# Projection in split halves from the sixth tile on, one row buffer for attention and norms, and three steps of each tile moved

## What is computed

```python
def attention(q, k, v, W_proj, b_proj):            # 16 heads of 32
    scores = einsum('bhqd,bhkd->bhqk', qh, kh) / sqrt(32)
    scores = where(abs(i - j) > 64, -inf, scores)  # window of 64 to each side
    y = einsum('bhqk,bhkd->bhqd', softmax(scores), vh)
    return y @ W_proj.T + b_proj

def ffn(x):                                        # scan over the 8 batches, c is 512 x 512
    f = sigmoid(x_t @ wf.T + c @ uf.T + bf)
    i = sigmoid(x_t @ wi.T + c @ ui.T + bi)
    g = tanh(x_t @ wc.T + c @ uc.T + bc)
    c = f * c + i * g                              # for each batch t
    return tanh(x @ wo.T + c_final @ uo.T + bo)

x = x + attention(layernorm(x), ctx, ctx, W_proj, b_proj)
x = x + ffn(layernorm(x))
```

## Time and profile before

| | |
|---|---|
| median of 3 runs | 1033.33 us |
| profiled execution, its own time | 1036.05 us |
| its span | 1034.3 us |
| PE, DVE, ACT, POOL busy | 97%, 59%, 47%, 18% |
| granted TensorE clock, mean | 0.991 of full |
| DMA | 99.36 MB, 96 GB/s over the span |

### The profile page before, as it was taken

One profiled execution on the slowest core, in us unless ns is written; L12 is line 12 of the kernel. 1 busy time (PEld: TensorE's weight loads), 2 busy tenths in 40 slices (PEclk: granted clock), 3 DMA queues, 4 the chain that ended last, 5 costly groups with the idle time before them and its releaser, 6 DMA issues.

```text
span 1034.3 us, 20027 instructions
## 1 busy us (share of the span) xinstructions
PE 1005.1 (97%) x6992; PEld 728.0 (70%) x6992; DVE 610.2 (59%) x2194; ACT 485.0 (47%) x1441; POOL 188.4 (18%) x289
## 2 busy tenths in 40 slices
PE   6998989999999999999999999999999999999997
PEld 4665656667776777767777777767777778888885
DVE  5757878776567755766676655765577632133222
ACT  6757656555454454554455445454454432131221
POOL 4535111101111111111111111111111000002354
PEclk9988999999999999999999999999999999999999
DMA  8346223222222122212222222211112003029666
GB/s 265 119 134 189 84 76 98 83 77 73 77 83 58 61 77 83 60 49 72 78 83 77 72 77 70 70 52 47 41 33 72 1 23 131 0 84 364 245 214 193
DMA packets 76244, 99.36 MB, mean 96 GB/s; under 512 B 5232, under 2 KB 46192, under 8 KB 74608
## 3 DMA queue, kind: packets, MB, share of 16 engines
q1 hardware_dynamic: 75424, 97.80, 29.7%
q10 hardware_dynamic: 720, 0.27, 0.1%
HBM read 68.69 MB, written 29.36 MB: 95 GB/s over the span
## 4 chain that ended last, share of the span: by engine, by line
PE 89%; DVE 4%; issue 2%; DMA 2%; ACT 1%; POOL 1%; SPq 0%; DVEq 0%; POOLq 0%; ACTq 0%
PE ps_g L474 16%; PE ps_g L472 16%; PE ps_g L473 16%; PE ps_m L569 12%; PE ps_a L508 6%; PE ps_a L527 4%; PE ps_v L548 3%; PE ps_m L575 2%; PE ps_v L553 2%; PE ps_g L520 2%; PE ps_m L562 2%; PE ps_a L472 1%; PE ps_a L473 1%; PE ps_a L474 1%; PE ps_m L483 1%
## 5 line engine op out<-in xcount | busy, mean ns | idle before, releaser
L727 DVE CUSTOM_DVE_ANT_0 probs<-ps_a,mask 128x192 f32<-128x192 f32 (+1 forms) x512 | 169.4, 387 | 193.1 <-PE ps_a L508 146.3
L641 ACT ACTIVATE probs<-probs,rowmin 128x192 f32<-128x192 f32 (+1 forms) x512 | 239.0, 471 | 1.8 <-DVE rowmin L727 1.8
L676 ACT ACTIVATE gate<-ps_g,bias 128x512 f32<-128x512 f32 x84 | 57.9, 689 | 216.7 <-PE ps_g L474 216.7
L750 DVE STREAM_TRANSPOSE probs_t<-probs 32x128 f32<-32x128 f32 x492 | 146.6, 298 | 6.0
L472 PE MATMUL ps_g<-state_hi,gate_w 128*128 128x512 f32 x336 | 145.5, 433 | 0.0
L646 ACT ACTIVATE probs_t<-ps_a 128x512 f32<-128x512 f32 x108 | 64.5, 597 | 153.6 <-PE ps_a L527 152.9
L474 PE MATMUL ps_g<-state_hi,gate_w 128*128 128x512 f32 x336 | 132.3, 394 | 0.0
L473 PE MATMUL ps_g<-state_lo,gate_w 128*128 128x512 f32 x336 | 131.2, 391 | 0.0
L456 POOL COPY recip<-invsum 128x128 f32<-128x128 f32 x128 | 38.5, 301 | 503.0 <-DVE invsum L734 503.0
L569 PE MATMUL ps_m<-wp,attn 128*128 128x512 f32 x256 | 121.6, 619 | 0.0
L641 ACT ACTIVATION_READ_ACCUMULATOR probs<-probs,rowmin 128x1 f32 x512 | 97.6, 191 | 0.0
(11 more groups left out here) (167 smaller groups left out, 1599.5 us busy)
## 6 DMA issues: line engine op xcount, KB each, us to landing
values<-ctx_rows SPq DMA_DIRECT2D x34, 256.0 KB, 4.3
xr<-x SPq DMA_DIRECT2D x32, 256.0 KB, 4.0
keys<-ctx_t SPq DMA_DIRECT2D x16, 512.0 KB, 4.0
x_dram<-xr SPq DMA_DIRECT2D x32, 256.0 KB, 4.2
gate_w<-x2t_dram SPq DMA_DIRECT2D x8, 1024.0 KB, 11.2
keys<-ctx_t SPq DMA_DIRECT2D x16, 384.0 KB, 3.4
x2t_dram<-x2t_even SPq DMA_DIRECT2D x12, 512.0 KB, 3.8
x2t_dram<-x2t_odd SPq DMA_DIRECT2D x12, 512.0 KB, 3.8
```

Of the source, the lines that this page charges most:

```text
L641: act.activation(row, row, ACT.Exp, bias=rowmin[:, i % 2, h:h + 1], scale=-1.0, accum_out=rowsum[:, i // G % 2, i % G, h:h + 1]).then_inc( ...
L676: act.activation(gate[:, min(gt, 1), :], ps_g[i % 2][:, :], ACT.Tanh, bias=(first_bias if b == 0 else bias)[:, gt, m:m + 1], scale=1.0 if ...
L727: dve.tensor_tensor_reduce(probs[:, i % 2, h, 0:SEEN[t]], ps_a[h][:, 0:SEEN[t]], mask[:, MASK0[t]:MASK0[t] + SEEN[t]], -SCALE, -NEG, ALU.a ...
L750: turn = dve.transpose(probs_t[BLK * keys_of:BLK * (keys_of + 1), HPG:2 * HPG, q], probs[q, i % 2, :, col:col + BLK])
```

## The change

Of the projections, those of tiles 5 to 31 (`WHOLE` is 5) are made in split halves. For that the projection's weights are split once, in slots 19 and 20 (`split_proj`: four ACT copies, four POOL subtractions), and each tile's attention is split behind `mult` (a new step `halves`: ACT rounds it into `attn_hi`, POOL subtracts into `attn_lo`). The raw projection weights lie where the recurrent state is kept later, so the first state waits for both. `xn`, `x2` and `attn` become one buffer, `tile_row`, and `queries` has one half only; the waits follow. In the later slots (n > 19) `query`, `turn2` and `spread` move from the end of slots 1, 2 and 3 to right behind `turn`, ACT's copy of the query stands behind `exp` as a step of its own (`query_out`), and `mult` goes from the start of the next tile to slot 3, in front of `exp` and `value`. `stat2` stands right behind `resid` in all slots (so in front of the maskings), and `ln2b` behind the `score` of slot 1.

```diff
@@ -56,6 +56,8 @@
 
     FIRST_CELL = G * TT + 3
     OWN_BANKS = FIRST_CELL + 1
+
+    WHOLE = OWN_BANKS // G
     XR = 4
     PAIR = 2
     chunks = [(gt, u, k) for u in (1, 0) for gt in range(NG) for k in range(0, G, PAIR)]
@@ -119,7 +121,7 @@
 
     steps += [("load_x", 0), ("load_k", 0), ("load_x", 1), ("load_v", 0), ("load_x", 2)]
     steps += [("load_k", 1), ("load_v", 1)]
-    steps += [("ln1", 0), ("ln1b", 0), ("bias", 0), ("query", 0), ("ln1", 1)]
+    steps += [("ln1", 0), ("ln1b", 0), ("bias", 0), ("query", 0), ("query_out", 0), ("ln1", 1)]
     steps += [("score", 0), ("score", 1), ("exp", 0), ("recip", 0)]
     split_slots = [1 + 3 * c // 2 for c in range(NCH)]
 
@@ -135,22 +137,29 @@
         if n + 1 in split_slots:
             steps.append(("load_w", split_slots.index(n + 1)))
         early = n <= FIRST_CELL
-        if s == 0 and n > FIRST_CELL + 1:
-            tile_steps("mult", i - 1)
         if s == 1 and early:
             tile_steps("resid", i - 1)
+            tile_steps("stat2", i - 1)
         if n < SLOTS:
             steps.append(("turn", n))
         if early:
             steps.append(("exp", n + 1))
         else:
+            if s > 0:
+                tile_steps((None, "query", "turn2", "spread")[s], (None, i + 1, i - 1, i)[s])
             cells(2)
         if n + 2 < SLOTS:
             steps.append(("score", n + 2))
+        if s == 1:
+            tile_steps("ln2b", i - 1)
+        if s == 3 and not early:
+            tile_steps("mult", i)
         if early:
             tile_steps(("proj", "query", "turn2", "spread")[s], (i - 1, i + 1, i - 1, i)[s])
         elif n + 1 < SLOTS:
             steps.append(("exp", n + 1))
+        if s == 1:
+            tile_steps("query_out", i + 1)
         if n < SLOTS:
             steps.append(("value", n))
         gates()
@@ -164,23 +173,18 @@
             if not early:
                 tile_steps("proj", i - 1)
                 tile_steps("resid", i - 1)
+                tile_steps("stat2", i - 1)
             tile_steps("load_k", i + 2)
             tile_steps("load_v", i + 1) if i > 0 else None
-        if s == 1:
-            tile_steps("stat2", i - 1)
-            if not early:
-                tile_steps("query", i + 1)
-            tile_steps("ln2b", i - 1)
         if s == 2:
-            if not early:
-                tile_steps("turn2", i - 1)
             tile_steps("load_x", i + 3)
             tile_steps("ln1", i + 2)
-        if s == 3:
-            if early:
-                tile_steps("mult", i)
-            else:
-                tile_steps("spread", i)
+        if s == 3 and early:
+            tile_steps("mult", i)
+        if s == 3 and i >= WHOLE:
+            tile_steps("halves", i)
+        if FIRST_CELL <= n < FIRST_CELL + 2:
+            steps.append(("split_proj", PAIR * (n - FIRST_CELL)))
         if n in split_slots:
             steps.append(("split", split_slots.index(n)))
         if n == 0:
@@ -227,18 +231,24 @@
         x2t = [x2t_even, x2t_odd]
         state_hi = sb("state_hi", [P, G, T], F32R)
         state_lo = sb("state_lo", [P, G, T], F32R)
-        wp = sb("wp", [P, G, D], F32)
+        proj_w = sb("proj_w", [P, 2, G, D], F32R)
+
+        wp = state
         xr = sb("xr", [P, XR, D], F32)
-        xn = sb("xn", [P, D], F32)
-        x2 = sb("x2", [P, D], F32)
-        queries = sb("queries", [P, 2, G, P], F32)
+
+
+        tile_row = sb("tile_row", [P, D], F32)
+        xn = x2 = tile_row
+        attn = tile_row[:, :].rearrange("p (g q) -> p g q", g=G)
+        queries = sb("queries", [P, G, P], F32)
         keys = sb("keys", [P, 2, G, KEYS], F32)
         values = sb("values", [P, 2, 2, D], F32)
         probs = sb("probs", [P, 2, HPG, KEYS], F32)
 
         probs_t = sb("probs_t", [P, 2 * HPG, P], F32)
         recip = sb("recip", [P, G, P], F32)
-        attn = sb("attn", [P, G, P], F32)
+        attn_hi = sb("attn_hi", [P, G, P], F32R)
+        attn_lo = sb("attn_lo", [P, G, P], F32R)
         gate = sb("gate", [P, 2, T], F32)
         mask = sb("mask", [P, MASKW], F32)
         ident = sb("ident", [P, P], F32)
@@ -450,6 +462,16 @@
                         pool.wait_ge(w_hi, PAIR * i + k - k0 + 1)
                         pool.tensor_tensor(gate_w[:, gt, u, 1, k, :], raw_w[i % RAW][:, k - k0, :],
                                            gate_w[:, gt, u, 0, k, :].bitcast(F32), ALU.subtract).then_inc(w_lo, 1)
+                if kind == "split_proj":
+                    for k in range(i, i + PAIR):
+                        pool.wait_ge(wp_hi, k + 1)
+                        pool.tensor_tensor(proj_w[:, 1, k, :], wp[:, k, :], proj_w[:, 0, k, :].bitcast(F32),
+                                           ALU.subtract).then_inc(wp_lo, 1)
+                if kind == "halves":
+                    pool.wait_ge(attn_round, i - WHOLE + 1)
+                    need(pool, projected, i)
+                    pool.tensor_tensor(attn_lo[:, :, :], attn, attn_hi[:, :, :].bitcast(F32), ALU.subtract)\
+                        .then_inc(attn_split, 1)
                 if kind == "recip":
                     pool.wait_ge(inverted, i + 1)
                     need(pool, spread, i // G)
@@ -505,7 +527,7 @@
                         mm.then_inc(column, 1)
                     for h in range(HPG):
                         rows = slice(HEAD * h, HEAD * (h + 1))
-                        mm = pe.matmul(ps_a[h][:, 0:seen], queries[rows, tile % 2, g, :], keys[rows, tile % 2, g, 0:seen],
+                        mm = pe.matmul(ps_a[h][:, 0:seen], queries[rows, g, :], keys[rows, tile % 2, g, 0:seen],
                                        start=True, stop=True)
                     mm.then_inc(scored, 1)
                 if kind == "turn":
@@ -564,9 +586,16 @@
                 if kind == "proj":
                     if i == 0:
                         pe.wait_ge(wp_in, DMA)
-                    pe.wait_ge(attn_t, i + 1)
-                    for k in range(G):
-                        mm = pe.matmul(ps_m[:, :], attn[:, k, :], wp[:, k, :], start=(k == 0), stop=(k == G - 1))
+                    if i < WHOLE:
+                        pe.wait_ge(attn_t, i + 1)
+                        for k in range(G):
+                            mm = pe.matmul(ps_m[:, :], attn[:, k, :], wp[:, k, :], start=(k == 0), stop=(k == G - 1))
+                    else:
+                        pe.wait_ge(wp_lo, G)
+                        pe.wait_ge(attn_split, i - WHOLE + 1)
+                        for k in range(G):
+                            mm = product(ps_m[:, :], (attn_hi[:, k, :], attn_lo[:, k, :]),
+                                         (proj_w[:, 0, k, :], proj_w[:, 1, k, :]), k == 0, k == G - 1)
                     mm.then_inc(projected, 1)
                 if kind == "turn2":
                     pe.wait_ge(x2_done, i + 1)
@@ -628,10 +657,10 @@
             for gt in range(NG):
                 act.dma_start(bias[:, gt, :], biases[gt]).then_inc(const_in, DMA)
             for kind, i in steps:
-                if kind == "query":
+                if kind == "query_out":
                     act.wait_ge(q_turned, i + 1)
-                    need(act, scored, G * (i - 1))
-                    act.activation(queries[:, i % 2], ps_m[:, :].rearrange("p (g q) -> p g q", g=G), ACT.Copy)\
+                    need(act, scored, G * i)
+                    act.activation(queries[:, :, :], ps_m[:, :].rearrange("p (g q) -> p g q", g=G), ACT.Copy)\
                        .then_inc(q_ready, 1)
                 if kind == "exp":
                     need(act, inverted, i - 2 * G + 1)
@@ -647,9 +676,16 @@
                        .then_inc(turned_a, 1)
                 if kind == "spread":
                     act.wait_ge(spread, i + 1)
+                    act.activation(attn, ps_m[:, :].rearrange("p (g q) -> p g q", g=G), ACT.Copy).then_inc(recip_out, 1)
+                if kind == "halves":
+                    act.wait_ge(attn_t, i + 1)
                     need(act, projected, i)
-                    act.activation(attn[:, :, :], ps_m[:, :].rearrange("p (g q) -> p g q", g=G), ACT.Copy)\
-                       .then_inc(recip_out, 1)
+                    act.activation(attn_hi[:, :, :], attn, ACT.Copy).then_inc(attn_round, 1)
+                if kind == "split_proj":
+                    if i == 0:
+                        act.wait_ge(wp_in, DMA)
+                    for k in range(i, i + PAIR):
+                        act.activation(proj_w[:, 0, k, :], wp[:, k, :], ACT.Copy).then_inc(wp_hi, 1)
                 if kind == "turn2":
                     b, t = i // TT, i % TT
                     act.wait_ge(x2_turned, i + 1)
@@ -708,6 +744,10 @@
                     r = i % 2
                     dve.wait_ge(rstd1, i + 1)
                     need(dve, q_turned, i)
+                    if i - 2 < WHOLE:
+                        need(dve, projected, i - 1)
+                    else:
+                        dve.wait_ge(attn_split, i - 1 - WHOLE)
```

(8 more changed lines are left out.)

2 lines of the change are left out of this document (added).

## The result

The changed kernel took 1020.35 us (median of 4 runs, 1014.17 to 1022.76), against 1034.05 us before: ratio 0.985 [0.982, 0.988], a gain of 13.7 us and not of 28.7. The time lies 3 us above the range. The four executions differ in the first 110 us above all: the profiled one is the fastest (1014.17 us, span 1012.4, mean clock 0.995), and the slowest (1022.76 us) has a clock of 0.990.

The account below looks back on a forecast made before the run. TensorE bounds the kernel, wholly so from 179 us; gains of 21.8 (third regime), 2.7 (second) and 4.2 us (first) make 28.7, taken from the profiled 1036.05 and lowered to the runs' median: 1005 us, range 995 to 1017.

Parts of the forecast that it names:

- Rival A: Third regime: new chain partly late, 0.3 to 0.8 us of each tile's 0.87 lost to waits; 1017 us, chance 0.15.
- rival C: Slower: mult too late, so mult, ACT and POOL come bare, 2.9 us per tile; 1076 us, chance 0.03.
- Rival D: Split products don't run in 0.23 us; from 0.30 us a step nothing is saved there; 1026 us, chance 0.03.
- 3.63 - 2.76 = 0.87 us per tile: Third regime (from 179 us): saving of the split projection, twelve rounded products at 2.76 us for the old 3.63.
- 20.9 us: Forecast gain from projection 8 to the end: projections 8 to 31, 24 x 0.87 us.
- 1.3 us for the third tile: First regime: weights land at 84.16, so the value product comes at 85.8 and not 87.13, gaining 1.3 us.
- 2.5 for the fourth: First regime: no transfer in the way, so the 1.84 us wait and 0.7 of low clock are gained.
- the second tile, where I set the gain to none: First regime: no gain, since ACT then stands 2.81 us for the weights' transfer.
- Rival B: Low clock of the first two regimes goes altogether and DVE's gaps close: 36 us gained, 998 us, chance 0.17.
- 3.6 forecast: Gain from projection 4 to 8: 2.7 us for the second regime and 0.87 of projection 7.
- about 1 us: Second regime: the early spread waits about 1 us for the maskings, blends and reciprocal of the slot before.
- 0.3 to 0.5 us to spare: Query's transposes behind the turn of slot 1: residual and norm of slot 0 ready 0.3 to 0.5 us ahead.

Follow-up runs that it names:

- `mult` late: Changed kernel with the spread back at the end of slot 3 and mult, then halves, at the start of the next tile: 1036.18 us, ratio 1.001.
- the cell that took them over: Changed kernel with one cell of slot 0 put between the value product and the split projection: 1020.76 us, ratio 0.987.
- the columns: Changed kernel with weights' transfers a slot earlier, and one first-bias column per score instead of two, started a slot earlier: 1007.00 us, ratio 0.972.
- the whole projection: Changed kernel with all projections in full precision, no weights or attention split, moved steps and shared row buffer kept: 1038.16 us, ratio 1.003.

## Why the prediction was wrong

**Right: where the gain lies, and that nothing of it is lost to waits in the third regime.** PE bounds the kernel, the split projection is nearly all of the gain (816 for 832 to 833 us; without it nothing), the halves hide behind the maskings and the value product, and the subtraction took 1.29 us for the estimated 1.27. Rival A, chain partly late, did not come: PE has no gap from 196 to 850 us. That the measured 1020.35 lies in rival A's range (1012 to 1025) is chance, since its mechanism is not there. Of rival C a late chain is real with `mult` late, at 0.5 us per tile and not 2.9, and the change avoids that place. Rival D is excluded by the steps of 0.23.

**Wrong by size: "3.63 - 2.76 = 0.87 us per tile".** The 2.76 was read off twelve products that begin behind the query's transposes, which had already paid for the passage from the narrow products. The projection stands right behind the narrow products, and what stood there in the profile before was the projection itself, so that the 3.63 held the passage and the 2.76 did not. The chain gives 2.95 us, a saving of 0.68; the way from projection 8 to the end gives 0.67 to 0.71 per tile, the length of a batch 0.66. Of 20.9 us that leaves 16.1 to 16.9. That the 0.20 belong to the place is shown by the cell that took them over; that they are the load of a 128-wide stationary operand which can't begin beside the 32-column products is what the load rows suggest, and no run shows it by itself. The Trainium skill (TensorE: Matmul & The Clock Gate, The mechanism) has a load run ahead beside a matmul when it goes to other rows of the array or to a background buffer; the loads beside the products of 0.23 us, each 0.39 us ahead, agree.

**Wrong in the first regime: 1.3 us for the third tile, 2.5 for the fourth.** This is the step that failed by its mechanism. The weights' transfers had been seen in the second tile, where I set the gain to none, and for the third ("the weights land at 84.16") I took their landing as fixed. I did not ask whether PE's next wait would be for them throughout. Measured were 3.0 us in one pair of profiles and none in the other, about 2 to 5 us lost by the medians, and undoing the move cost nothing. By the medians this is the largest part of what is missing from the 28.7. With the transfers a slot earlier the move is worth 6.2 us. The low clock, which I counted as won back with the wait (0.7 of the 2.5), came behind the waits that took its place as well. Rival B, low clock gone altogether, needed the early transfers and the columns: 99.36 us at projection 4 for 107.25.

**Wrong by size in the second regime: 3.6 forecast, 2.0 measured.** The forecast had the spread wait for the reciprocals "about 1 us" in one tile; it waits 0.65 us in each of four, and the query's turn, given "0.3 to 0.5 us to spare", was late twice. Of the 2.0 us a part is not the change's: with early transfers alone the kernel before takes 89.0 us there, since its projection 5 then no longer falls into the low clock. The changed kernel's 88.7 are 0.3 better than that. With the whole projection the same order takes 91.2, so the moves cost 2.2 us and the split gives back 2.5. With the query and the spread behind the cells these waits are gone.

**The DVE and POOL exchange.** `ln2b`, now away from POOL's weight subtractions, takes 0.55 us at 96.62 us, for the 1.48 of the earlier trace rows. In the worst slot POOL's subtraction waits, through the reciprocal, for the blends to end, so the two don't meet. But the rows have what the forecast found only for `ln2b`. Where DVE splits the state, with both inputs in SBUF, POOL's root beside it takes 0.93 us for the 0.55 it takes otherwise (so in the kernel before too), and the one subtraction that begins beside a blend takes 1.73 us for 1.29, while the blend keeps its 0.69 (timelines after):

```profile
297.89 0.93 POOL L452 TENSOR_TENSOR rs<-ve,half 128x1 f32<-128x1 f32 x1 [1.82 <-DVE ve L742]
...
326.47 0.55 POOL L452 TENSOR_TENSOR rs<-ve,half 128x1 f32<-128x1 f32 x1 [2.63 <-DVE ve L742]
...
824.33 1.73 POOL L473 TENSOR_TENSOR attn_lo<-tile_row,attn_hi 128x512 fp32r<-128x512 f32 x1 [5.99 <-ACT attn_hi L683]
```

```profile
297.72 1.89 DVE L859 SCALAR_TENSOR_TENSOR state_lo<-state,state_hi 128x512 fp32r<-128x512 f32 x3
...
824.21 0.69 DVE L848 SCALAR_TENSOR_TENSOR state<-gate 128x512 f32<-128x512 f32 x1
```

The Trainium skill (SBUF — State Buffer, Who interferes with whom) has the rule that a DVE instruction with two inputs there and a GpSimd one that reads there exclude each other; these rows agree with it. PE waited for none of them, so it adds nothing to the sum.

## What to carry to other kernels

Read the price of an instruction from a row that has the same neighbour in front of it as the new place will have: 0.2 us per tile, read off a run of equal products in the middle of a stream, were 4 to 5 us in all. Before counting a wait as gained, name what the waiting engine will wait for next and whether that is earlier by as much: two late arrivals at the same place hide each other, and an edit that looks like nothing, or like a loss, may be worth 8 us beside the other. A step put directly behind another engine's result wants work in front of it; a step hidden in one regime may be bare in the one before it.

## What the runs showed of the hardware

- A 128x512 product of rounded operands directly behind the narrow value products adds 0.43 us to the chain instead of 0.23, and four 128x128 transposes 0.59 us instead of 0.44.
- PE can fall to a lower clock without having waited. Behind two groups of sixteen one-column matmuls the granted clock of three microseconds was 0.62, with PE shown busy 100% of them. In the second execution of the kernel before it was at 0.50 (1.2 GHz) from 55.2 to 75.7 us, with PE busy throughout and no wait since one of 0.32 us at 39.5. So a full busy share does not say that the clock will hold. With single columns it stayed at 1.00 up to the last microseconds; what of that edit does it is open.
- A GpSimd instruction beside a VectorE instruction with both inputs in SBUF takes longer, by 0.37 us (0.93 for 0.55) and 0.44 us (1.73 for 1.29), and the VectorE instruction does not.
- Two executions of the changed kernel differ by 5.6 us at projection 4 (107.25 and 112.80). Of these 1.6 us are there at projection 0. Behind it the transfers land later (ACT's wait 2.11 or 3.37 us), PE waits 1.01 or 2.28 us, and the clock is at 0.50 for 6.8 us in the first and for 13.7 us in the second.
